# Weighing two key tiles in one block of TensorE, with a fourth buffer of probabilities

## Chip, cores and metric

One core of one Trainium2 chip. The metric is the device time of one execution of the whole program in microseconds (us). Engines: PE is TensorE's matmuls, PEld its weight loads, DVE is VectorE, ACT ScalarE, POOL GpSimd, SP the queue that issues most transfers.

## What is computed

Four transformer layers on x (8 batches x 256 tokens x 128 channels), each an attention and a feed-forward net, with a context of 8 x 1601 tokens x 64 channels. The first and the fourth layer hold a cross attention with 16 heads of 8 channels over all 1601 context tokens:

```python
Q = (x @ Wq.T).reshape(B, 256, 16, 8);  K, V = (z @ Wkv.T) as (B, 1601, 16, 8) each
attn = softmax(einsum('bqhd,bkhd->bhqk', Q, K) * 8 ** -0.5, axis=-1)
O = einsum('bhqk,bkhd->bqhd', attn, V)
```

These two cross attentions are what the change touches; the rest (self attentions, an attention with 16 heads of 32, one with a single head, the feed-forward nets) stays.

## The kernel before

`split_cross` (from line 1772) runs one such attention. It is called twice: for layer 0 with its first queries and keys made ahead, and for layer 3, where it makes its queries itself. The work is cut into 32 **groups** (`NG`): 8 batches of 4 groups with 4 heads each. The 1601 keys of a group are 13 **tiles** (`KT`) of up to 128 keys; a tile of a group is a step u, 416 in all. For every u:

- *fill, scores* (line 1938): four matmuls, one per head, write a tile's scores (128 keys x 256 queries for each head) to one of two score buffers in PSUM. Queries and keys are cut into bf16 pieces, so that the contraction is over 50 rows; two heads lie in the two halves of TensorE's rows.
- *drain, exponential* (line 2018): ScalarE writes exp of the 1024 scores per key to a buffer of probabilities, `probs`; there are three, taken in turn by u. Before it, it waits until the weigh of u-3 is done.
- *weigh* (line 1971): four matmuls in f32, one per head, contract 128 keys: 9 columns of weights (8 value channels and a one, whose sum is the softmax's denominator) against 256 queries. The four heads lie at columns 0, 32, 64 and 96 of the array. The profile shows each as two passes, so a weigh is x8. They add up in one PSUM bank over the 13 tiles of a group.

The softmax's maxima are searched in a pass ahead: *max* (line 1953) multiplies queries by keys the other way round, 32 maxima tiles of 401 keys per group, some 8 steps ahead of the group's own scores; VectorE reduces each (line 2074) from one of two PSUM buffers, the ring: one of two banks, which takes two tiles at once, and one of one bank, used in turn. The maxima are put together (line 2079), cut into bf16 pieces on GpSimd (2115, 2117), transposed on TensorE (*neg*, line 1923), copied by ScalarE (2011) and sent by SP to two further rows of the queries. After a group's last weigh ScalarE copies its output (*take*, 2027), TensorE transposes it (*turn*, 1979), and VectorE divides (2090, 2095). Keys and values of the next batch are projected between (`kproj`, line 1910; `vproj`, line 1916), the keys' pieces cut on GpSimd.

The order is written by a planner, `split_plan` (from line 1687), one list for all engines; each engine runs its own steps of it in that order, with semaphores. A slot is one fill (scores, or a projection, or neg). `LENGTH` gives the planned length of each kind of step; `done` adds these up for two points of each slot, after its fill and after its weigh, and the 32 maxima tiles of a group are put where that sum has reached equal shares. In a slot i the plan runs: fill i, other steps, maxima of the first point, the weigh of the tile that was filled in slot i-2, maxima of the second point, drain of slot i-1.

```python
        if i >= 2 and slots[i - 2][1][0] == "scores":
            u = slots[i - 2][1][1]
            plan.append(("weigh", u))
```

Of the kernel before, what the change touches and what calls it, by code (L numbers as in the profile page):

```python
# [17 lines left out]
ACT = mybir.ActivationFunctionType  # L18
# [4 lines left out]
P = 128  # L23
B = 8
S = 256
# [6 lines left out]
KT = -(-LC // P)  # L32
# [1516 lines left out]
NG = B * GT  # L1549
PER = KT * GT  # L1550
LEAD = 8
LENGTH = dict(scores=0.25, weigh=0.6, qproj=0.9, kproj=0.9, vproj=1.0, neg=0.25)
KT_IN = 16 * 2 * PIECES


# [131 lines left out]
def split_plan(ready):  # L1687

    slots, steps = [], [(-89.0, ("ones",)), (-90.0 if ready else -69.7, ("ctx", 1))]
    if not ready:
        slots += [(-80.0, ("qproj", 0))] + [(-71.0 + c, ("qproj", c)) for c in range(1, 4)]
        steps += [(-69.9, ("qsplit", 0)), (-69.8, ("qsend", 0)), (3, ("qsplit", 1))]
        steps += [(36 + 2.9 * i, ("qsend", 1, i)) for i in range(2 * PIECES)]
    for b in range(B):
        at = PER * (b - 1)  # L1700
        if b >= 2:
            steps.append((at - 34, ("ctx", b)))
        if b >= 1:
            first, apart = (at - 9.5, 1.5) if b == 1 else (at - 22.5, 1)
            slots += [(first + apart * c, ("kproj", b, c)) for c in range(4)]
            steps += [(first + 5.5 + 2.4 * i, ("ksplit", b, i)) for i in range(4)]
            for a in range(GT):
                steps += [(first + 15.5 + 8 * a + 0.65 * i, ("ksend", b, a, i)) for i in range(2 * PIECES)]
        first, apart = (-19.5, 2) if b == 0 else (at + 9.5, 1)
        slots += [(first + apart * s, ("vproj", b, s)) for s in range(5)]  # L1710
    for n in range(NG):
        lo = KT * (n - 1) - LEAD
        hi = lo + KT
        steps += [(hi, ("place", n)), (hi + 0.1, ("cut", n)), (hi + 4.6, ("negsend", n))]
        slots.append((hi + 4.5, ("neg", n)))
    slots = sorted(slots + [(u, ("scores", u)) for u in range(NG * KT)], key=lambda e: e[0])
    steps.sort(key=lambda e: e[0])
    done, work = [], 0.0
    for i, (_, step) in enumerate(slots):
        work += LENGTH[step[0]]  # L1720
        done.append([work])
        if i >= 2 and slots[i - 2][1][0] == "scores":
            work += LENGTH["weigh"]
        done[i].append(work)
    points = [(i, half) for i in range(len(slots)) for half in range(2)]
    items = {point: [] for point in points}
    for n in range(NG):
        lo = KT * (n - 1) - LEAD
        begin, end = [next(i for i in range(len(slots)) if i + 1 == len(slots) or slots[i + 1][0] - 1 > t)
                      for t in (lo, lo + KT)]  # L1730
        mine = [point for point in points if begin <= point[0] < end]
        low, high = done[begin - 1][1] if begin else 0.0, done[end - 1][1]
        for item in range(32):
            at = low + (high - low) * (item + 0.5) / 32
            items[next(point for point in mine if done[point[0]][point[1]] >= at)].append(("max", n, item))
    plan, turns = [], []
    for i, (_, step) in enumerate(slots):
        until = slots[i + 1][0] - 1 if i + 1 < len(slots) else 1e9
        plan.append(("fill",) + step)
        while steps and steps[0][0] < until:  # L1740
            plan.append(steps.pop(0)[1])
        plan += items[i, 0] + turns
        turns = []
        if i >= 2 and slots[i - 2][1][0] == "scores":
            u = slots[i - 2][1][1]
            plan.append(("weigh", u))
            if u % KT == KT - 1:
                turns = [("turn", u // KT)]
        plan += items[i, 1]
        if i:  # L1750
            plan.append(("drain",) + slots[i - 1][1])
        if turns:
            plan.append(("take", turns[0][1]))
    last = NG * KT - 1
    plan += [("weigh", last - 1), ("drain", "scores", last), ("weigh", last), ("take", NG - 1), ("turn", NG - 1)]
    slot = {step: i for i, (_, step) in enumerate(slots)}
    out, ring, skip = [], {}, False
    for step in plan:
        if step[0] == "max":
            if skip:  # L1760
                skip = False
                continue
            wide = len(ring) % 2 == 0 and step[2] < 31
            step = step + (2 if wide else 1,)
            skip = wide
        if step[0] in ("max", "turn"):
            ring[step] = len(ring)
        out.append(step)
    return out, slot, ring


def split_cross(nc, k, scale, tiles, ctx_t, xt, wq, wk, wv, y):

    plan, slot, ring = split_plan(wq is None)
# [4 lines left out]
    with ExitStack() as ctx:  # L1779
        def sb(name, shape, dt=F32):  # L1780
            return k.sb(name, shape, dt, ctx)
# [2 lines left out]
        kt = (tiles.kt0, sb("kt1", [P, GH, LC], BF16))  # L1784
        qf = y.rearrange("p t c -> p (t c)")
        v = sb("v_cur", [P, 2, KT, H * 9])
        pr = sb("probs", [P, 3, 4 * S])
        ot = sb("ot", [P, S])
        rden = sb("rden", [P, QT, 4])
        mx, negm = sb("mx", [P, 2, 32]), sb("negm", [P, 2, 8])  # L1790
# [13 lines left out]
        def wait(eng, sem, count):  # L1804
            if count > 0:
                eng.wait_ge(sem, count)
# [86 lines left out]
        def _(pe):  # L1893
            for step in plan:
                kind = step[0]
                if kind == "fill":
                    kind, of = step[1], step[1:]
                    pair = spair(of)
# [20 lines left out]
                    elif kind == "neg":  # L1919
                        n = of[1]  # L1920
# [21 lines left out]
                elif kind == "max":  # L1942
                    n, i0, count = step[1], step[2], step[3]
                    b, a = n // GT, n % GT
                    if i0 == 0:
                        wait(pe, kt_in[b % 2][a], KT_IN * (b // 2) + KT_IN * (b % 2))
                        if wq is not None:
                            pe.wait_ge(q_in[0 if b < 2 else 1], 16 * 2 * PIECES)
                    wait_ring_reuse(pe, step)
                    for i in range(count):  # L1950
                        j, g, tok, lo = item(n, i0 + i)
                        rows = slice(CC * j, CC * j + PROWS)
                        ins = pe.matmul(bank(step, i)[:, 0:CH], qs[rows, g, tok:tok + P],  # L1953
                                        kt[b % 2][rows, g, lo:lo + CH], start=True, stop=True)
                    ins.then_inc(ring_full, 1)
                elif kind == "weigh":
                    u = step[1]
                    n, t = u // KT, u % KT
                    b, a = n // GT, n % GT
                    m = min(P, LC - P * t)  # L1960
                    if t == 0:
                        if a == 0:
                            wait_drained(pe, ("vproj", b, 4))
                        if n == 0:
                            pe.wait_ge(o_clear, 1)
                        wait(pe, taken, n)
                    wait_drained(pe, ("scores", u))
                    for jj in range(4):
                        j, h = jj % 2, 4 * a + jj
                        at = 2 * S * j + S * (jj // 2)  # L1970
                        ins = pe.matmul(obank[32 * jj:32 * jj + 9, :], v[0:m, b % 2, t, 9 * h:9 * h + 9],  # L1971
                                        pr[0:m, u % 3, at:at + S], start=(t == 0), stop=(t == KT - 1))
                    ins.then_inc(pv_done, 1)
                elif kind == "turn":
                    n = step[1]
                    pe.wait_ge(taken, n + 1)
                    wait_ring_reuse(pe, step)
                    for i in range(QT):
                        ins = pe.transpose(bank(step)[:, P * i:P * i + P], ot[:, P * i:P * i + P], k.ident[:])
                    ins.then_inc(ring_full, 1)  # L1980

        @block.scalar
        def _(act):
            for step in plan:
                kind = step[0]
                if kind == "drain":
# [20 lines left out]
                    elif kind == "neg":  # L2007
                        n = of[1]
                        wait(act, neg_in[n % 2], 32 * (n // 2))
                        wait_filled(act, of)  # L2010
                        act.activation(sg[:, n % 2, :], pair[:, 0, :].bitcast(BF16)[0:8, 0:S],
                                       ACT.Copy).then_inc(s_free, 1)
                    else:
                        u = of[1]
                        m = min(P, LC - P * (u % KT))
                        wait(act, pv_done, u - 2)
                        wait_filled(act, of)
                        act.activation(pr[0:m, u % 3, :], pair[0:m].rearrange("p a n -> p (a n)"), ACT.Exp,  # L2018
                                       scale=scale).then_inc(s_free, 1)
                elif kind == "qsend" and step[1] == 0:  # L2020
                    send_queries(act, 0, (1,))
# [1158 lines left out]
```

## Time and profile before

| | us |
|---|---|
| median of 3 runs | 3841.56 (3839.25 to 3856.53) |
| the profiled execution | 3862.31 |
| its span in the trace | 3860.5 |
| TensorE, VectorE, ScalarE, GpSimd busy in the span | 3281.6, 2320.5, 1797.2, 1139.3 |
| first attention with heads of 8, about | 355 to 974 |
| second, about | 3085 to 3743 |

Busy shares are averages over stages with different limits, so the two attentions are read by themselves. Matmuls are pipelined and their ends are modelled: the start of one against the start of the next tells more than how long one seems to last. An instruction that waits is put down to the semaphore that came last.

### The profile page before, as it was taken

The page shows a single profiled execution, that of the slowest core. Times are in us where ns is not written, and L with a number is a line of the kernel's source. Part 1 is how long each engine was busy: PE and PEld are TensorE (multiplying, and loading weights), DVE is VectorE, ACT ScalarE, POOL GpSimd, SP SyncE. Part 2 cuts the span into 40 slices and gives each one's busy share as a digit, 9 for nine tenths or more (in the row PEclk, how much of TensorE's full clock was granted, in tenths as well). Part 3 has the DMA queues.
Part 4 walks back from the last instruction along what each step waited for, and adds up shares of the span by engine and source line. Part 5 has one row for each costly group of instructions (what it writes and reads, how often), then busy time and mean ns, then how long its engine had stood idle before and what let it go on. Part 6 is the DMA issues. An engine that isn't in the chain of part 4 may idle for free. (4 is left out here: it accounts for less than half of the span.)

```text
span 3860.5 us, 80811 instructions
## 1 busy us (share of the span) xinstructions
PE 3281.6 (85%) x33476; PEld 1659.7 (43%) x33476; DVE 2320.5 (60%) x3829; ACT 1797.2 (47%) x2204; POOL 1139.3 (30%) x797
## 2 busy tenths in 40 slices
PE   6898999999589837999999999978787599999986
PEld 4663333333366523444444444445454233333334
DVE  4455788888466453555555555533334577778876
ACT  2332777778133322444444444443221066777762
POOL 2001111110233252655556655662101121111103
PEclk9996999999599857999999999998887688999987
DMA  4200211110100021000000000000211222121100
GB/s 66 26 2 17 52 32 35 42 42 4 31 9 2 1 60 26 10 2 10 10 10 1 10 10 2 2 1 2 56 47 22 41 49 46 38 46 33 27 2 11
DMA packets 68751, 90.05 MB, mean 23 GB/s; under 512 B 36990, under 2 KB 49322, under 8 KB 68394
## 3 DMA queue, kind: packets, MB, share of 16 engines
q1 hardware_dynamic: 67962, 84.58, 10.8%
q8 instruction: 262, 4.29, 0.5%
q14 instruction: 95, 0.78, 0.1%
q10 hardware_dynamic: 432, 0.39, 0.0%
HBM read 34.31 MB, written 4.33 MB: 10 GB/s over the span
## 5 line engine op out<-in xcount | busy, mean ns | idle before, releaser
L2074 DVE TENSOR_REDUCE mx<-ps 128x2 f32<-128x802 f32 (+1 forms) x1372 | 1020.7, 777 | 251.7 <-PE ps L1953 230.2
L2018 ACT ACTIVATE probs<-ps 128x1024 f32<-128x1024 f32 (+1 forms) x832 | 826.8, 1024 | 210.1 <-PE ps L1938 204.3
L2386 DVE TENSOR_REDUCE mx<-ps 128x3 f32<-128x1203 f32 (+1 forms) x352 | 483.0, 1372 | 478.6 <-PE ps L2282 478.6
L2434 POOL TENSOR_TENSOR sums<-sums,probs 128x2048 f32<-128x2048 f32 x128 | 579.2, 4525 | 143.8 <-ACT probs L2361 129.4
L1971 PE MATMUL ps<-probs,v_cur 128*9 128x256 f32 x6656 | 549.0, 401 | 0.5 <-ACT probs L2018 0.5
L2361 ACT ACTIVATE probs<-ps 128x1024 f32<-128x1024 f32 x384 | 372.2, 1021 | 357.8 <-PE ps L2260 357.7
L1953 PE MATMUL ps<-kt,qs 48*128 48x401 bf16 x2048 | 484.8, 362 | 52.2 <-DVE mx L2074 36.9
L1938 PE MATMUL ps<-qs,kt 50*128 50x256 bf16 (+1 forms) x3328 | 388.1, 288 | 12.4 <-DMA qs<-max_rows 10.1
L2282 PE MATMUL ps<-kt,qt 32*128 32x401 f32 x2048 | 340.2, 556 | 46.7 <-DVE mx L2386 41.1
L1953 PEld LDWEIGHTS ps<-kt,qs 48*128 48x128 bf16 x2048 | 129.3, 95 | 505.2 <-DVE mx L2074 279.6
L2115 POOL CAST max_pieces<-negm 128x8 bf16<-128x8 f32 x64 | 12.2, 191 | 1083.4 <-DVE negm L2079 1083.4
L2260 PE MATMUL ps<-qt,kt 32*128 32x256 f32 (+1 forms) x3328 | 251.7, 375 | 0.0
L2303 PE MATMUL ps<-probs,v_cur 128*32 128x256 f32 (+1 forms) x3328 | 226.9, 386 | 12.9 <-issue 12.7
L1938 PEld LDWEIGHTS ps<-qs,kt 50*128 50x128 bf16 (+1 forms) x3328 | 165.9, 100 | 134.0 <-issue 51.2
L2282 PEld LDWEIGHTS ps<-kt,qt 32*128 32x128 f32 x2048 | 110.9, 186 | 200.9 <-DVE mx L2386 117.4
L2260 PEld LDWEIGHTS ps<-qt,kt 32*128 32x128 f32 (+1 forms) x3328 | 188.5, 181 | 12.1
L844 ACT ACTIVATE probs<-ps 128x768 f32<-128x768 f32 (+1 forms) x128 | 110.4, 914 | 172.1 <-PE ps L777 93.9
L1971 PEld LDWEIGHTS ps<-probs,v_cur 128*9 128x9 f32 x6656 | 103.1, 89 | 184.4 <-issue 130.8
L2303 PEld LDWEIGHTS ps<-probs,v_cur 128*32 128x32 f32 (+1 forms) x3328 | 87.3, 109 | 135.0 <-issue 98.6
L2255 PE MATMUL ps<-max_rows,ones_b 2*128 2x512 bf16 (+1 forms) x896 | 106.2, 371 | 35.7 <-ACT probs L2361 21.7
L878 DVE RECIPROCAL rden<-ps 128x256 f32<-128x256 f32 x64 | 112.3, 1754 | 38.1 <-PE ps L788 38.1
L2431 POOL COPY sums<-probs 128x2048 f32<-128x2048 f32 x32 | 60.5, 1891 | 230.3 <-ACT probs L2361 230.3
(399 smaller groups left out, 4292.0 us busy)
## 6 DMA issues: line engine op xcount, KB each, us to landing
kt<-k SPq DMA_DIRECT2D x680, 50.0 KB
ctx_s<-in_ctx_t SPq DMA_DIRECT2D x16, 400.2 KB, 4.7
ctx_s<-ctx_norm_t SPq DMA_DIRECT2D x16, 400.2 KB, 5.3
kt<-k SPq DMA_DIRECT2D x24, 200.1 KB
ctx_norm_t<-ctx_norm_t SPq DMA_DIRECT2D x8, 400.2 KB, 3.8
ctx_a<-in_ctx_t SPq DMA_DIRECT2D x8, 400.2 KB, 4.2
ctx_b<-in_ctx_t SPq DMA_DIRECT2D x8, 400.2 KB
qs<-q SPq DMA_DIRECT2D x12, 256.0 KB
```

The lines of the kernel that those rows point to most:

```text
L878: dve.reciprocal(rden[:], lbank).then_inc(divided, 1)
L1938: ins = pe.matmul(pair[0:m, j, S * (jj // 2):S * (jj // 2) + S], kt[b % 2][rows, g, P * t:P * t + m], qs[rows, g, S * b:S * b + S], start= ...
L1953: ins = pe.matmul(bank(step, i)[:, 0:CH], qs[rows, g, tok:tok + P], kt[b % 2][rows, g, lo:lo + CH], start=True, stop=True)
L1971: ins = pe.matmul(obank[32 * jj:32 * jj + 9, :], v[0:m, b % 2, t, 9 * h:9 * h + 9], pr[0:m, u % 3, at:at + S], start=(t == 0), stop=(t == ...
L2018: act.activation(pr[0:m, u % 3, :], pair[0:m].rearrange("p a n -> p (a n)"), ACT.Exp, scale=scale).then_inc(s_free, 1)
L2074: dve.tensor_reduce(mx[:, n % 2, i0:i0 + count], src, AX_X, ALU.max).then_inc(freed(step), 1)
L2260: ins = pe.matmul(sbanks[0:m, j, S * i:S * i + S], kt[rows(j), n % 4, P * t:P * t + m], qt[rows(j), b % 2, a, :], start=False, stop=(i == ...
L2282: ins = pe.matmul(rbanks[:, i - 3 * i0, 0:CH], qt[rows(j), b % 2, a, q:q + P], kt[rows(j), n % 4, lo:lo + CH], start=True, stop=True)
L2303: ins = pe.matmul(obank[rows(j), :], v[0:m, n % 2, t, rows(j)], pr[0:m, (NW * n + w) % NPR, j, i, :], start=(t == 0), stop=(t == KT - 1))
L2361: ins = act.activation(pr[:, u % NPR, 2 * f:2 * f + 2, :, :].rearrange("p j i n -> p (j i n)"), sbanks[:, 2 * f:2 * f + 2, :].rearrange("p ...
L2386: dve.tensor_reduce(mx[:, n % 2, 3 * i0:3 * i0 + count], rbanks[:, 0:count, 0:CH], AX_X, ALU.max).then_inc(ring_free, 1)
L2434: pool.tensor_tensor(o, o, p, ALU.add).then_inc(added, 1)
```

## The change

The planner collects tiles that may be weighed in a list and weighs two at once, in one slot, when two are there; when the second belongs to the next group, the first is weighed alone. In slots between, no tile is weighed. A double block is planned at twice 0.45 and 0.15 for a change of the array's shape, where each weigh was planned at 0.6. The probabilities get a fourth buffer (`NPS`), so the exponential of u waits for the weigh of u-4.

```diff
--- before.py
+++ after.py
@@ -1549,7 +1549,8 @@
 NG = B * GT
 PER = KT * GT
 LEAD = 8
-LENGTH = dict(scores=0.25, weigh=0.6, qproj=0.9, kproj=0.9, vproj=1.0, neg=0.25)
+NPS = 4
+LENGTH = dict(scores=0.25, weigh=0.45, turnround=0.15, qproj=0.9, kproj=0.9, vproj=1.0, neg=0.25)
 KT_IN = 16 * 2 * PIECES
 
 
@@ -1715,12 +1716,21 @@
         slots.append((hi + 4.5, ("neg", n)))
     slots = sorted(slots + [(u, ("scores", u)) for u in range(NG * KT)], key=lambda e: e[0])
     steps.sort(key=lambda e: e[0])
+    weighs, ready = [], []
+    for i in range(len(slots)):
+        if i >= 2 and slots[i - 2][1][0] == "scores":
+            ready.append(slots[i - 2][1][1])
+        now = ready[:2] if len(ready) >= 2 else []
+        if now and now[1] % KT == 0:
+            now = now[:1]
+        ready = ready[len(now):]
+        weighs.append(now)
     done, work = [], 0.0
     for i, (_, step) in enumerate(slots):
         work += LENGTH[step[0]]
         done.append([work])
-        if i >= 2 and slots[i - 2][1][0] == "scores":
-            work += LENGTH["weigh"]
+        if weighs[i]:
+            work += LENGTH["weigh"] * len(weighs[i]) + LENGTH["turnround"]
         done[i].append(work)
     points = [(i, half) for i in range(len(slots)) for half in range(2)]
     items = {point: [] for point in points}
@@ -1741,8 +1751,7 @@
             plan.append(steps.pop(0)[1])
         plan += items[i, 0] + turns
         turns = []
-        if i >= 2 and slots[i - 2][1][0] == "scores":
-            u = slots[i - 2][1][1]
+        for u in weighs[i]:
             plan.append(("weigh", u))
             if u % KT == KT - 1:
                 turns = [("turn", u // KT)]
@@ -1752,6 +1761,7 @@
         if turns:
             plan.append(("take", turns[0][1]))
     last = NG * KT - 1
+    plan += [("weigh", u) for u in ready if u < last - 1]
     plan += [("weigh", last - 1), ("drain", "scores", last), ("weigh", last), ("take", NG - 1), ("turn", NG - 1)]
     slot = {step: i for i, (_, step) in enumerate(slots)}
     out, ring, skip = [], {}, False
@@ -1784,7 +1794,7 @@
         kt = (tiles.kt0, sb("kt1", [P, GH, LC], BF16))
         qf = y.rearrange("p t c -> p (t c)")
         v = sb("v_cur", [P, 2, KT, H * 9])
-        pr = sb("probs", [P, 3, 4 * S])
+        pr = sb("probs", [P, NPS, 4 * S])
         ot = sb("ot", [P, S])
         rden = sb("rden", [P, QT, 4])
         mx, negm = sb("mx", [P, 2, 32]), sb("negm", [P, 2, 8])
@@ -1969,7 +1979,7 @@
                         j, h = jj % 2, 4 * a + jj
                         at = 2 * S * j + S * (jj // 2)
                         ins = pe.matmul(obank[32 * jj:32 * jj + 9, :], v[0:m, b % 2, t, 9 * h:9 * h + 9],
-                                        pr[0:m, u % 3, at:at + S], start=(t == 0), stop=(t == KT - 1))
+                                        pr[0:m, u % NPS, at:at + S], start=(t == 0), stop=(t == KT - 1))
                     ins.then_inc(pv_done, 1)
                 elif kind == "turn":
                     n = step[1]
@@ -2013,9 +2023,9 @@
                     else:
                         u = of[1]
                         m = min(P, LC - P * (u % KT))
-                        wait(act, pv_done, u - 2)
+                        wait(act, pv_done, u - NPS + 1)
                         wait_filled(act, of)
-                        act.activation(pr[0:m, u % 3, :], pair[0:m].rearrange("p a n -> p (a n)"), ACT.Exp,
+                        act.activation(pr[0:m, u % NPS, :], pair[0:m].rearrange("p a n -> p (a n)"), ACT.Exp,
                                        scale=scale).then_inc(s_free, 1)
                 elif kind == "qsend" and step[1] == 0:
                     send_queries(act, 0, (1,))
```

## Rows read from the trace of the kernel before

**Rows 1.** Busy time by stretch; columns: stretch, length, each engine (instructions), granted clock, DMA.

```profile
355.00:974.00 619.00, 591.18 (x6316) 207.76 (x6316) 503.61 (x780) 459.42 (x537) 72.96 (x88) 0.96 0.15 33
3085.00:3743.00 658.00, 618.22 (x6335) 213.08 (x6333) 508.39 (x785) 462.89 (x541) 87.63 (x94) 0.91 0.18 35
400.00:950.00 550.00, 525.71 (x5683) 186.77 (x5682) 470.49 (x728) 412.38 (x483) 68.03 (x80) 0.98 0.15 35
3100.00:3340.00 240.00, 222.90 (x2120) 76.43 (x2117) 176.07 (x271) 154.02 (x184) 34.24 (x35) 0.85 0.26 46
```

**Rows 2.** Engines over the whole span: busy us (share), instructions; the profile page.

```profile
PE 3281.6 (85%) x33476; PEld 1659.7 (43%) x33476; DVE 2320.5 (60%) x3829; ACT 1797.2 (47%) x2204; POOL 1139.3 (30%) x797
```

**Rows 3.** Groups by line, 400 to 950 us: count | busy us, mean ns | idle before.

```profile
L2018 ACT ACTIVATE probs<-ps 128x1024 f32<-128x1024 f32 (+1 forms) x372 | 370.6, 1022 | 75.4 <-PE ps L1938 72.4
...
L1971 PEld LDWEIGHTS ps<-probs,v_cur 128*9 128x9 f32 (+1 forms) x2967 | 45.7, 88 | 77.1 <-issue 52.9 <-ACT probs L2018 21.6 <-ACT kf L1998 2.5
...
L2074 DVE TENSOR_REDUCE mx<-ps 128x2 f32<-128x802 f32 x303 | 299.8, 989 | 39.4 <-PE ps L1953 36.0
L2074 DVE TENSOR_REDUCE mx<-ps 128x1 f32<-128x401 f32 x310 | 176.4, 571 | 36.5 <-PE ps L1953 30.8
...
L2090 DVE RECIPROCAL rden<-ps 128x8 f32<-128x8 f32 x29 | 5.9, 202 | 1.0
```

**Rows 4.** Timeline, 603.1 to 607 us: start, us, engine, line, operation, count, [idle before].

```profile
603.25 0.12 PEld L1971 LDWEIGHTS ps<-probs,v_cur 128*9 128x9 f32 x8 [0.21 <-ACT probs L2018]
...
603.80 0.34 PE L1953 MATMUL ps<-kt,qs 48*128 48x401 bf16 x1
...
604.26 0.34 PE L1953 MATMUL ps<-kt,qs 48*128 48x401 bf16 x2
...
604.54 0.62 PE L1971 MATMUL ps<-probs,v_cur 128*9 128x256 f32 x8
...
606.13 0.34 PE L1953 MATMUL ps<-kt,qs 48*128 48x401 bf16 x2
...
606.59 0.99 DVE L2074 TENSOR_REDUCE mx<-ps 128x2 f32<-128x802 f32 x1 [0.38 <-PE ps L1953]
```

**Rows 5.** Timeline of PE, 3718.3 to 3719.3 us, and from 3719.05 us (second pass alone).

```profile
3718.14 0.34 PE L1953 MATMUL ps<-kt,qs 48*128 48x401 bf16 x2
3718.32 0.38 PE L1938 MATMUL ps<-qs,kt 50*128 50x256 bf16 x4
3718.63 0.62 PE L1971 MATMUL ps<-probs,v_cur 128*9 128x256 f32 x8
...
3718.86 0.40 PE L1971 MATMUL ps<-probs,v_cur 128*9 128x256 f32 x4
```

**Rows 6.** Timeline of PE, 477.5 to 479.0 us.

```profile
477.55 0.34 PE L1953 MATMUL ps<-kt,qs 48*128 48x401 bf16 x2
477.83 0.22 PE L1923 MATMUL ps<-identb,max_pieces 128*8 128x128 bf16 x1
...
478.47 0.34 PE L1953 MATMUL ps<-kt,qs 48*128 48x401 bf16 x1
```

**Rows 7.** Timeline of the first attention's tail, 962.1 to 964.5 us.

```profile
961.11 3.77 ACT L2018 ACTIVATE probs<-ps 128x1024 f32<-128x1024 f32 x4
...
963.10 0.39 PE L1938 MATMUL ps<-qs,kt 50*128 50x256 bf16 x4
...
964.02 0.39 PE L1938 MATMUL ps<-qs,kt 50*128 50x256 bf16 x4
```

**Rows 8.** Waits, 400 to 950 us: us in total, times, longest.

```profile
PEld ps L1953 <- DVE mx L2074: 122.8, 292, 0.7
...
PE ps L1953 <- DVE mx L2074: 12.5, 46, 0.6
```

**Rows 9.** Busy time around a fall of the clock, columns as in Rows 1.

```profile
459.50:466.90 7.40, 6.59 (x65) 3.10 (x65) 5.58 (x11) 4.17 (x8) 0.00 (x0) 1.00 0.32 71
466.90:473.70 6.80, 6.80 (x53) 1.99 (x49) 3.33 (x5) 4.39 (x5) 0.00 (x0) 0.50 0.56 128
```

## The prediction

> **What bounds the kernel now.** The table of windows comes first, because the change touches two stretches alone: the two attentions with 16 heads of 8. They take 619 and 658 us of the 3860.5 us span [rows 1], and in them TensorE is busy for 591 and 618 us, against 60% for the whole-span share of VectorE and 47% of ScalarE [rows 2]. In the even part, 400 to 950 us, TensorE is busy for 525.7 of 550 us, VectorE for 470.5 (85.5%), ScalarE for 412.4 (75%), at a granted clock of 0.98 [rows 1]. So TensorE sets the pace there, VectorE follows at 14 points' distance, and no other engine is near. In the second attention the stretch from 3100 to 3340 has less of both clock (0.85) and load [rows 1].
>
> The groups by line, for 400 to 950 us, name VectorE's work: 303 reductions of two tiles at 0.989 us, and 310 of one at 0.571 us; ScalarE has 372 exponentials of 1.02 us [rows 3]. The division of a group's output occurs 29 times [rows 3], so a group (13 key tiles) takes 550/29 = 19.0 us. What VectorE waits for is the maxima's matmuls, 36.0 of 39.4 us idle ahead of the wide reductions and 30.8 of 36.5 ahead of the narrow ones [rows 3].
>
> The timeline then shows how TensorE spends a slot. A weigh starts at 603.25 and the next work of another shape at 603.80: 0.55 us [rows 4]. But its second pass starts 0.23 us after its first (3718.63, 3718.86) [rows 5], so its two passes stream for about 0.44 us, and **0.11 us** goes by before the next maxima matmul. On the way in, a maxima pair at 604.26 is followed by a weigh at 604.54, 0.28 us later [rows 4], where the same pair ahead of a scores block, no change of shape, takes 0.18 us (3718.14 to 3718.32) [rows 5]: **0.10 us** more. So a weigh costs 0.44 us and two pauses, 0.21 us together. That these pauses belong to the change of the array's shape and not to every block is seen where the maxima's transposes (128 rows by 8 columns, shaped like a weigh) stand directly ahead of one: entry at 477.83, 0.28 us after the pair as always, next maxima at 478.47 [rows 6]. The 0.64 us hold both transposes and the weigh, 0.09 more than a weigh alone; a second pair of pauses does not fit into 0.09.
>
> **The change, part by part.** *Fewer blocks.* Two tiles wait until they can be weighed together, but the last tile of a group stands alone (13 is odd): 7 blocks for 13 tiles in place of 13, 6 fewer. Two attentions of 32 groups: 6 x 64 = 384 pairs of pauses. At 0.21 us that is **81 us** of TensorE's time, on the engine that sets the pace.
>
> *The joint inside a double block.* The trace of before has no two weighs back to back without a wait. From below: nothing, as between the passes inside one, where all eight weight loads lie in the first 0.12 us of the block [rows 4]. From above: one weight load in the open, 0.088 us by the mean of its row [rows 3]. I take nothing, since the second four loads are hidden behind the first pass already; the other end goes into the range, and is a rival.
>
> *The later weigh.* The first of two tiles is weighed a slot later. Who waits for it is ScalarE, for a buffer of probabilities: with four, the exponential of tile u needs the weigh of u-4, which stands in the block before. Cost nothing; cover: a whole slot. A copy of a group's output (ScalarE) and its transposes also come a slot later, and move along with the block; the first weigh of the next group waits for that copy as before. Nothing is queued on SP or POOL by the moved step: a weigh issues no transfer.
>
> *Two fills of scores without a weigh between them.* There are two score buffers, so a fill needs the exponential two back. ScalarE alone, in the tail without maxima, does one in 0.92 to 0.94 us (four in 3.77; fills at 963.10 and 964.02) [rows 7]. Two make 1.88 us, while a pair of slots takes 550/186 = 2.96 us all told; with 0.2 us less it is 2.75. So ScalarE stays covered, except in that tail, some 8 slots at each attention's end, where TensorE already goes at ScalarE's pace and gains nothing (4 of 208 pairs, 1.5 us).
>
> *New weights of the planner.* 32 maxima tiles per group are spread by planned work. Per two slots the plan is now 0.25 + 0.25 for fills and 0.9 + 0.15 for the double block, so of some four maxima tiles about 2.7 stand right behind the block, 0.6 behind each fill. The number of matmuls is unchanged; what changes is how even VectorE's supply is. That is the term which gives back.
>
> *What is late next.* VectorE. In 400 to 950 us, 29 x 6 = 174 pairs of pauses, 36.5 us, go away; its idle time falls from 79.5 to 43 us [rows 1]. TensorE now stands idle for 550 - 525.7 = 24.3 us there [rows 1], about half of it shown as waiting for a maxima buffer (12.5 us) [rows 8]. If this wait grows as VectorE's slack shrinks, 79.5/43 = 1.85 times, it becomes 45 us: 20.6 of the 36.5 us saved are given back, 56%. The other end is that none is. I take a third, nearer to none than that estimate, because part of the 24.3 us are waits of fixed length (for ScalarE's copy ahead of the transposes), that do not grow.
>
> *The sum.* 81 x 2/3 = 54 us, from the profiled execution's 3862.3 us (span 3860.5, 1.8 around it): 3808. The median of the runs shown, 3841.56, is 0.9946 of that execution: **3788 us**, 1.4% less. The ends: 81 us (3761) and 81 x 0.44 = 36 us (3806).
>
> **The rivals.** *No give-back:* VectorE's ring stays filled and 81 us arrive, 3761. For it: VectorE would be at 470.5/513.5 = 92%, not full. Against it: it already idles for want of work while TensorE waits for it, so the two are not in step.
>
> *Loads in the open.* Within one weigh the second loads lie under the first pass [rows 4], but all matmuls of a weigh use all 128 rows. If the first load of the second weigh stood open, a joint would cost 0.088 us, and 384 x (0.21 - 0.088) = 47 us would be saved, less a third: 31, so 3811. The Trainium skill, TensorE: Matmul & The Clock Gate, section Part 3 (packing small matmuls), says that a weight load overlaps matmuls in flight only where the row group differs, which speaks for this rival. By that rule the eight loads of one weigh could not lie together under its own first pass either; the trace has them there, so I give it little.
>
> *The ring eats it.* TensorE reaches the maxima after a double block in a bunch, finds both buffers full, and waits as long as it saved: within 0.5% of 3842 (0.5% is about what a measurement of this kernel can tell from no change). For it: there are but two buffers, and already now 292 maxima loads were released last by a reduction [rows 8]. Against: VectorE has 14 points to give before it bounds.
>
> *VectorE runs dry in each double block, slower.* The place is the last maxima step ahead of a block. Reduction starts 0.46 us after its matmul (606.13, 606.59) [rows 4]. The next one comes 0.28 (entry) + 0.88 (two weighs) + 0.11 + 0.46 us after that matmul: 1.27 us from start to start. If only that one step is in the ring, VectorE has 0.99 or 0.57 us of work in it and stands dry for 0.28 or 0.70 us, 0.49 in the mean. A pair of slots holds 470.5/186 = 2.53 us of VectorE's work and 0.43 us of its idle time now. So it decides from 0.43 us of idle time per pair: at 0.49 the pair takes 3.02 against 2.96 us, +0.06 x 384 = 24 us, 3886, by medians 3865. For it: only 0.6 tiles stand ahead of a block. Against: the ring holds two steps, up to 1.56 us of work, and a step that had to wait for its buffer is issued late, with the earlier one still in work.
>
> *Granted clock.* It falls to its lower level, 1.2 GHz, for 6.8 us after the projections of the values (from 466.9; in the 7.4 us before, TensorE was busy for 6.59) [rows 9]. Whether fewer pauses spare some of these I cannot tell; it is in the range, not in the sum.
>
> **How the numbers follow.** The forecast with its give-back 0.50; no give-back 0.12; loads in the open 0.09; ring eats it 0.18; slower 0.11. The first three are faster by over 0.5% (below 3822): 0.71. Within: 0.18. Slower: 0.11. The range takes in the first three and half of the fourth: from somewhat under 3761, for the clock, 3752, to 3838.
>
> **What would show it.** In the changed kernel's timeline 16 weigh matmuls stand together, the second eight 0.44 us after the first (0.53 with a load in the open), the block 1.0 us long to the next shape. The even stretch's group takes 18.1 us in place of 19.0, VectorE's share there is about 90%, the attentions are some 27 us shorter each. Wrong would be: a joint over 0.1 us; VectorE's share at or under 85% with maxima reductions idle for matmuls more than 76 us in 550; TensorE's wait for maxima buffers two times 12.5 us or more; ScalarE idle for a weigh.

## The result: slower, and the profile after

The changed kernel takes 3943.6 us (median of 4) against 3840.4 us: a ratio of **1.0252**, 95% interval 1.0209 to 1.0295, so 103 us (80 to 113) are lost. Its profiled execution has a span of 3928.1 us, the lowest of its runs, where that of before was among the highest of its own; the two traces differ by less than the medians do.

Busy time by stretch in the changed kernel, columns as in [rows 1]: both attentions, from and to the same points of their work as there (6312 and 6335 matmuls, against 6316 and 6335), and 400 to 950 us.

```profile
358.00:1034.00 676.00, 587.03 (x6312) 233.29 (x6310) 501.78 (x780) 451.71 (x537) 72.47 (x88) 0.94 0.14 31
3129.00:3811.00 682.00, 583.04 (x6335) 232.75 (x6333) 505.80 (x784) 456.16 (x541) 87.64 (x94) 0.95 0.17 34
400.00:950.00 550.00, 478.42 (x5085) 191.60 (x5085) 418.79 (x648) 364.10 (x437) 66.81 (x74) 0.94 0.16 34
```

The attentions have grown from 619 and 658 us to about 676 and 682. TensorE is not busier but idler: 478 of 550 us in place of 525.7. VectorE fell from 85.5% to 76%, ScalarE from 75% to 66%. All three engines wait more, and for each other. The mean granted clock of the two attentions, 0.94 and 0.95 against 0.96 and 0.91, moved in both directions, and the groups below that have 1.00 in both kernels lose all the same (5.9 of 6.3 us): it is not the cause.

The same lines by group and the waits, 400 to 950 us of the changed kernel (its line numbers are 10 higher; beside [rows 3] and [rows 8]):

```profile
L2028 ACT ACTIVATE probs<-ps 128x1024 f32<-128x1024 f32 (+1 forms) x332 | 325.0, 1022 | 103.4 <-PE ps L1948 102.4
L2084 DVE TENSOR_REDUCE mx<-ps 128x2 f32<-128x802 f32 x268 | 265.1, 989 | 60.3 <-PE ps L1963 58.5
L2084 DVE TENSOR_REDUCE mx<-ps 128x1 f32<-128x401 f32 x279 | 158.6, 570 | 67.2 <-PE ps L1963 64.2
```

```profile
PE ps L1963 <- DVE mx L2084: 45.8, 102, 1.0
...
PE ps L1948 <- ACT probs L2028: 13.6, 22, 1.0
```

The mean of each instruction is what it was. But TensorE's wait for a maxima buffer rose from 12.5 to 45.8 us while VectorE's wait for maxima rose from 66.8 to 122.7 us; its wait for a score buffer is now 13.6 us, and ScalarE's for scores rose from 72.4 to 102.4 us. Each engine waits for another that waits for it: the buffers between them are handed over at the wrong times.

One cycle of two slots, timeline of the changed kernel, 610 to 613.2 us:

```profile
610.06 0.55 PEld L1981 LDWEIGHTS ps<-probs,v_cur 128*9 128x9 f32 x16 [0.28 <-issue]
610.06 1.05 PE L1981 MATMUL ps<-probs,v_cur 128*9 128x256 f32 x16
...
611.05 0.51 PE L1963 MATMUL ps<-kt,qs 48*128 48x401 bf16 x3
...
611.23 0.55 PE L1948 MATMUL ps<-qs,kt 50*128 50x256 bf16 x4
611.50 1.47 DVE L2084 TENSOR_REDUCE mx<-ps 128x2 f32<-128x802 f32 x2 [0.39 <-PE ps L1963]
...
612.64 0.35 PE L1963 MATMUL ps<-kt,qs 48*128 48x401 bf16 x2 [0.86 <-DVE mx L2084]
...
612.81 0.40 PE L1948 MATMUL ps<-qs,kt 50*128 50x256 bf16 x4
...
613.14 1.05 PE L1981 MATMUL ps<-probs,v_cur 128*9 128x256 f32 x16
```

The double block (x16) takes 0.99 us to the next shape, as forecast, and all its weight loads lie in its first 0.55 us. Behind it TensorE issues three maxima tiles, a pair and a single, which fill both buffers, and a fill. Its third step needs the pair's buffer again. VectorE, which had run dry for 0.39 us, starts on the pair at 611.50, and TensorE stands for 0.86 us until 612.64. The cycle takes 3.08 us.

In other cycles a fill stands. Here two fills follow each other at once (x8), and the next waits 0.97 us for an exponential:

```profile
601.10 0.60 PE L1948 MATMUL ps<-qs,kt 50*128 50x256 bf16 x8
...
602.66 0.39 PE L1948 MATMUL ps<-qs,kt 50*128 50x256 bf16 x4 [0.97 <-ACT probs L2028]
```

What I had averaged over shows in the four groups of one batch, one row each from division to division. First the kernel before, then the changed kernel:

```profile
545.30:562.90 17.60, 17.28 (x197) 5.89 (x199) 13.23 (x21) 14.25 (x16) 0.39 (x2) 0.90 0.29 63
562.90:585.20 22.30, 21.19 (x214) 6.99 (x213) 19.41 (x31) 15.95 (x21) 9.90 (x6) 1.00 0.07 15
585.20:602.60 17.40, 16.42 (x200) 5.46 (x192) 16.28 (x26) 13.68 (x16) 0.40 (x2) 1.00 0.10 22
602.60:623.40 20.80, 19.87 (x213) 8.58 (x207) 17.12 (x28) 14.47 (x19) 0.39 (x2) 1.00 0.26 56
```

```profile
565.50:583.50 18.00, 16.01 (x192) 6.17 (x192) 12.52 (x21) 13.46 (x16) 0.39 (x2) 0.92 0.26 56
583.50:608.50 25.00, 20.93 (x215) 7.64 (x218) 19.90 (x31) 16.01 (x21) 9.90 (x6) 1.00 0.06 14
608.50:627.60 19.10, 15.01 (x194) 6.20 (x190) 15.38 (x26) 13.61 (x16) 0.40 (x2) 1.00 0.09 21
627.60:649.90 22.30, 20.68 (x221) 9.82 (x213) 17.95 (x28) 14.36 (x20) 0.40 (x2) 1.00 0.26 56
```

Before, VectorE is busy for 16.28 of 17.40 us of the third group and for 19.41 of 22.30 us of the second, but for 13.23 of 17.60 us of the first. In the third group VectorE sets the time, though TensorE looks as busy: with short reductions it takes 15.7 us (e2, below). The change lost 0.4, 2.7, 1.7 and 1.5 us: 6.3 us per batch, about the whole loss if all 16 batches (two attentions of 8) lose as much.

Where VectorE's time in the third group goes is seen in its own timeline. Before, it stands idle for maxima three times, 0.78 us in all:

```profile
585.87 3.00 DVE L2074 TENSOR_REDUCE mx<-ps 128x2 f32<-128x802 f32 x4 [0.15 <-PE ps L1953]
589.24 0.99 DVE L2074 TENSOR_REDUCE mx<-ps 128x2 f32<-128x802 f32 x1 [0.38 <-PE ps L1953]
...
595.59 7.10 DVE L2074 TENSOR_REDUCE mx<-ps 128x2 f32<-128x802 f32 x9 [0.25 <-PE ps L1953]
```

In the changed kernel it does so seven times, 3.4 us in all, about once for each of the seven blocks of weighs; three of the seven:

```profile
614.57 1.96 DVE L2084 TENSOR_REDUCE mx<-ps 128x1 f32<-128x401 f32 x3 [0.40 <-PE ps L1963]
617.13 2.50 DVE L2084 TENSOR_REDUCE mx<-ps 128x2 f32<-128x802 f32 x3 [0.60 <-PE ps L1963]
620.42 2.98 DVE L2084 TENSOR_REDUCE mx<-ps 128x1 f32<-128x401 f32 x4 [0.79 <-PE ps L1963]
```

### The profile page after: what moved, and what is told of

Read it like the earlier page. It is cut to its first block and busy times, and to the rows that moved or that the text cites. A ratio compares the mean times of both kernels' runs of the same rounds, so it can differ in the third digit from the quotient of the medians.

```text
span 3928.1 us, 80805 instructions
## 1 busy us (share of the span) xinstructions
PE 3227.9 (82%) x33476; PEld 1698.4 (43%) x33476; DVE 2314.7 (59%) x3827; ACT 1783.4 (45%) x2204; POOL 1139.4 (29%) x797
## 5 line engine op out<-in xcount | busy, mean ns | idle before, releaser
L2028 ACT ACTIVATE probs<-ps 128x1024 f32<-128x1024 f32 (+1 forms) x832 | 815.4, 1023 | 271.1 <-PE ps L1948 267.3
L1963 PE MATMUL ps<-kt,qs 48*128 48x401 bf16 x2048 | 451.2, 359 | 137.2 <-DVE mx L2084 123.7
L1981 PE MATMUL ps<-probs,v_cur 128*9 128x256 f32 x6656 | 475.7, 402 | 0.4 <-ACT probs L2028 0.4
L1948 PE MATMUL ps<-qs,kt 50*128 50x256 bf16 (+1 forms) x3328 | 367.7, 283 | 46.8 <-ACT probs L2028 35.7
L1963 PEld LDWEIGHTS ps<-kt,qs 48*128 48x128 bf16 x2048 | 119.1, 94 | 514.0 <-DVE mx L2084 265.5
L1981 PEld LDWEIGHTS ps<-probs,v_cur 128*9 128x9 f32 x6656 | 144.7, 92 | 190.4 <-issue 90.9
```

The source lines that it names most:

```text
L1948: ins = pe.matmul(pair[0:m, j, S * (jj // 2):S * (jj // 2) + S], kt[b % 2][rows, g, P * t:P * t + m], qs[rows, g, S * b:S * b + S], start= ...
L2028: act.activation(pr[0:m, u % NPS, :], pair[0:m].rearrange("p a n -> p (a n)"), ACT.Exp, scale=scale).then_inc(s_free, 1)
```

## Experiments

Two theories of the loss: **the ring** (the planner bunches the maxima behind the double block, and two buffers can't carry VectorE over it), and **the score buffers** (two fills stand close together, the second waits for the exponential two back). Ratios are to the kernel before on the same chip, with 95% intervals.

**Taking VectorE out of the way** (e1 changed, e2 before): the reductions read 64 columns, about 0.23 us each.

```diff
-                        src = k.ps[:, 4:6, 0:CH]
+                        src = k.ps[:, 4:6, 0:64]
-                        src = bank(step)[:, 0:CH].rearrange(...)
+                        src = bank(step)[:, 0:64].rearrange(...)
-                                       scale=scale).then_inc(s_free, 1)
+                                       scale=scale / 8).then_inc(s_free, 1)
```

> The changed kernel, with VectorE's maxima reductions cut to 64 of their 401 columns (and exponents scaled by 1/8, so that they stay finite): VectorE's ring is out of the way, TensorE and ScalarE have all their work. Ring theory (TensorE waits for VectorE because the maxima stand in a bunch behind the double block): the saved pauses show, 60 to 80 us below the kernel before with the same cut (e2), about 3710 to 3740 us. Score buffer theory (the second of two fills close together waits for the exponential two back): nothing gained against e2, at or above it, about 3790 us or more.

> The kernel before with the same cut of the reductions. Both theories: only its own waits for the ring go, some 24 us of 550 in the even stretch, so 3780 to 3820 us.

Measured: e1 0.9757 (0.9713 to 0.9801), 3754.6 us; e2 **0.9690** (0.9650 to 0.9729), 3729.7 us. The sizes of both expectations missed; e1 above e2 is what the score buffer theory said. The kernel before is 119 us faster with shorter reductions, not the 25 to 65 that were expected. The four groups of the batch in e2, to set beside those of the kernel before above (there the first has a granted clock of 0.90, the others 1.00):

```profile
518.60:534.70 16.10, 15.94 (x197) 5.54 (x201) 4.84 (x22) 14.19 (x18) 0.39 (x2) 1.00 0.37 73
534.70:555.50 20.80, 20.46 (x210) 7.03 (x206) 7.07 (x31) 15.42 (x20) 9.71 (x6) 1.00 0.06 14
555.50:571.20 15.70, 15.62 (x196) 5.55 (x192) 5.97 (x26) 13.61 (x16) 0.60 (x3) 1.00 0.09 21
571.20:590.90 19.70, 19.69 (x211) 8.46 (x203) 6.21 (x26) 14.76 (x20) 0.40 (x2) 1.00 0.28 61
```

They take 72.3 us in place of 78.1, 5.8 less, where TensorE's visible idle time in the batch was 3.35 us (78.1 - 74.75): VectorE held it for more than the profile shows as waiting. That is 93 us for 16 such batches; the rest of the 119 us is not shown to be VectorE's, since the mean granted clock of e2's runs was higher too (0.917 to 0.919, against 0.900 to 0.914). With VectorE out of the way the changed kernel is still 0.7 points (26 us) above. So of 103 us lost, the reductions' length is needed for about 77. The rest fits the score buffers, whose wait is seen in e1 (first row; 400 to 900 us) and not in e2 (second):

```profile
PE ps L1948 <- ACT probs L2028: 24.8, 46, 1.0
```

```profile
PE ps L1938 <- ACT probs L2018: 1.6, 8, 0.3
```

**Taking ScalarE out of the way** (e5 changed, e6 before), and both (e7 changed, e8 before): the exponential covers half its columns.

```diff
-                        act.activation(pr[0:m, u % NPS, :], pair[0:m].rearrange("p a n -> p (a n)"), ACT.Exp,
+                        act.activation(pr[0:m, u % NPS, 0:2 * S], pair[0:m, 0, :], ACT.Exp,
+            dve.memset(pr[:], 1.0).then_inc(o_clear, 1)
...
```

> The changed kernel with each exponential cut to half (512 of 1024 columns, the other half of the probabilities stays 1.0; two heads in four are so left out), VectorE's reductions whole: fills no longer wait for ScalarE, the ring stays as it is. Score buffer theory: most of the loss goes, level with e6 or up to 40 us below it. Ring theory: the loss stays, 50 us or more above e6.

> The kernel before with the same half exponentials (two heads in four left out). Both theories: it hardly waited for ScalarE, 0.5 us in the even stretch, so 3820 to 3845 us.

> The changed kernel with both cuts (64 of 401 columns reduced, half the exponentials; so maxima and two heads in four are not the reference's): TensorE alone is left. Both theories: the 384 pairs of pauses show in full, 65 to 85 us below e8. If a double block does not save its pauses, level with e8.

> The kernel before with both cuts (64 of 401 columns reduced, half the exponentials). Both theories: as e2, 3715 to 3735 us, since nothing there waited for ScalarE.

Measured: e5 1.0126 (1.0085 to 1.0167), e6 0.9951 (0.9921 to 0.9980): 1.75 points apart, so shorter exponentials take a third off the loss, and 67 us stay, as the ring theory said (50 or more). e7 **0.9654** (0.9594 to 0.9715), e8 **0.9632** (0.9585 to 0.9679): level, against both theories' 65 to 85 us. Yet in single cycles the pauses are saved. Two slots with the same work, two maxima steps (three tiles), two fills and two weighs, timeline of e8 and then e7 (e7's rows start two cycles ahead):

```profile
643.72 0.62 PE L1971 MATMUL ps<-probs,v_cur 128*9 128x256 f32 x8
...
645.80 0.40 PE L1971 MATMUL ps<-probs,v_cur 128*9 128x256 f32 x4
```

```profile
645.13 0.51 PE L1963 MATMUL ps<-kt,qs 48*128 48x401 bf16 x3
...
645.58 0.46 DVE L2087 TENSOR_REDUCE mx<-ps 128x1 f32<-128x64 f32 x2 [0.79 <-PE ps L1963]
645.86 0.09 PEld L1963 LDWEIGHTS ps<-kt,qs 48*128 48x128 bf16 x1 [0.28 <-DVE mx L2087]
...
648.80 1.05 PE L1981 MATMUL ps<-probs,v_cur 128*9 128x256 f32 x16
...
650.67 0.62 PE L1981 MATMUL ps<-probs,v_cur 128*9 128x256 f32 x8
```

2.08 us in e8 (643.72 to 645.80), 1.87 us in e7 (648.80 to 650.67): 0.21 less. But two cycles ahead of it, e7's maxima matmul of 645.13 is reduced from 645.58 on, in 0.23 us, and its buffer is refilled at 645.86: a round trip of 0.73 us, 0.5 us of it the matmul itself and the two hand-overs (0.45 us to the reduction's start, 0.05 us from its end). In the bunch behind a double block that is too long even for a tiny reduction. In the planner's list of the kernel before, a weigh (0.55 us) stands between two uses of a buffer of the ring in all but 84 of 716 cases; in that of the changed kernel in all but 289 of 715.

**Hardly any maxima** (e9 changed, e10 before): both cuts, and 4 of 32 maxima tiles.

```diff
-        for item in range(32):
-            at = low + (high - low) * (item + 0.5) / 32
+        for item in range(4):
+            at = low + (high - low) * (item + 0.5) / 4
...
```

> The changed kernel with both cuts and with 4 of the 32 maxima tiles of a group (the other maxima stay 0; 28 of 32 maxima matmuls and reductions and two heads in four are left out): almost no buffer of the ring is needed twice within a block's time. If double blocks save their pauses and the ring's round trip took them back (e7 level with e8): 65 to 90 us below e10. If a double block saves nothing over the whole kernel: level with e10.

> The kernel before with the same omissions (4 of 32 maxima tiles, 64 columns reduced, half the exponentials). Some 18 maxima steps of 0.17 us fewer in each of 64 groups than e8: about 200 us below it, 3490 to 3540 us.

Measured: e9 0.9425 (0.9370 to 0.9479), e10 0.9457 (0.9409 to 0.9506); 13 us apart by medians, the intervals overlap: not the 65 to 90 expected, and both (3608 and 3621 us) far above 3540 us. Another wait had taken the place, of the first scores of a group for the maxima's rows from SP (e9, 400 to 800 us, below; 17.2 us in e10), and the granted clock of 400 to 700 us was 0.87 and 0.89, where e7 and e8 have 1.00. So these two do not tell the theories apart.

```profile
PE ps L1948 <- DMA qs<-max_rows: 24.8, 16, 3.3
```

**Spreading the maxima otherwise** (e3 even; e4 at the points of the kernel before).

```diff
-LENGTH = dict(scores=0.25, weigh=0.45, turnround=0.15, ...
+LENGTH = dict(scores=0.52, weigh=0.2, turnround=0.11, ...            (e3)
+LENGTH = dict(scores=0.25, weigh=0.6, ...                            (e4)
-        if weighs[i]:
-            work += LENGTH["weigh"] * len(weighs[i]) + LENGTH["turnround"]
+        if i >= 2 and slots[i - 2][1][0] == "scores":                (e4)
+            work += LENGTH["weigh"]
```

> The changed kernel with other planned lengths (0.52 a fill, 0.2 a weigh, 0.11 the change of shape), so that of a pair of slots' maxima a third stands behind the first fill, a third behind the double block, a third behind the second fill, in place of 0.6, 2.7 and 0.6 tiles. Ring theory: the waits for VectorE fall to those of the kernel before or less, 3780 to 3810 us. Score buffer theory: the two fills are as close as they were in work, still over 3880 us.

> The changed kernel with the maxima at the points of the kernel before (each weigh counted with 0.6 in its old slot): in a pair of slots 0.6 tiles ahead of the double block, 1.4 behind it, 2.0 behind the second fill. Ring theory: between e3 and the changed kernel, 3800 to 3860 us. Score buffer theory: two more tiles between the close fills, so some 30 us better than the changed kernel, 3900 us or more.

Measured: e3 **1.0092** (1.0061 to 1.0124), 3884 us; e4 1.0252 (1.0211 to 1.0294), 3952.6 us, as slow as the changed kernel. The even spread alone, with the same pairs, wins back 1.6 points, 61 us of 103. But neither run came out as the ring theory had it, and 3884 and 3952.6 us are within the score buffer theory's numbers (over 3880, over 3900), though it also said that e4 would be 30 us better than the changed kernel. TensorE's waits tell more, 400 to 900 us of e3 (two rows), then of e4:

```profile
PE ps L1963 <- DVE mx L2084: 30.4, 67, 0.8
PE ps L1948 <- ACT probs L2028: 7.6, 15, 0.6
```

```profile
PE ps L1963 <- DVE mx L2084: 55.3, 121, 0.8
```

The changed kernel has 42.4 and 12.4 us there, the kernel before 11.1 for the ring. In e4 the wait for a score buffer is gone and the loss is not: it stands at the ring. Why, can be counted in the planner's lists. Of some 710 times that a buffer of the ring is used again in an attention, no weigh and at most one fill stands since its last use 62 times before, 158 times in the changed kernel, 183 in e4 and 80 in e3: e4's spread moved the bunch to another place. What is left in e3 was asked of the next two.

**The even spread with the cuts** (e13 both; e14 exponentials alone): e3's `LENGTH` in e7 and in e5.

> As e7 (both cuts: 64 of 401 columns reduced, half the exponentials), with the even spread of e3. If what keeps e7 level with e8 is the round trip of a maxima buffer, needed again too soon in the bunch behind a double block: 30 to 70 us below e8, about 0.945 to 0.955 of the kernel before, where e8 is 0.963. If double blocks lose in some other way: level with e7, 0.965.

> As e5 (half the exponentials, VectorE's reductions whole), with the even spread of e3. If the bunch alone made TensorE wait for VectorE: level with e6 or below it, 0.985 to 0.997 of the kernel before. If VectorE's share by group is the limit, which no spread within a group mends: between e6 and e5, 1.000 to 1.010.

Measured: e13 **0.9524** (0.9477 to 0.9571), 1.1 points (some 41 us) below e8, as the round trip of a maxima buffer had it (30 to 70), and 1.3 below e7: the spread alone turned level into gain, of half the 81 us. e14 1.0084 (1.0049 to 1.0118), no better than e3, as was expected if VectorE's share by group is the limit: with an even spread ScalarE no longer matters, against the score buffer theory, and pairing still loses while the reductions are whole. The third group of the batch, in e8, e7, e13, and then e14:

```profile
554.80:570.30 15.50, 15.41 (x196) 5.71 (x192) 5.94 (x25) 8.15 (x16) 0.89 (x3) 1.00 0.10 22
```

```profile
556.90:573.00 16.10, 15.23 (x194) 6.03 (x198) 5.49 (x25) 8.19 (x16) 0.40 (x2) 1.00 0.09 21
```

```profile
552.00:567.10 15.10, 14.56 (x196) 6.59 (x192) 5.82 (x25) 8.09 (x16) 0.40 (x2) 1.00 0.11 24
```

```profile
585.00:603.80 18.80, 15.70 (x192) 6.47 (x188) 16.44 (x26) 7.90 (x15) 0.40 (x2) 0.97 0.13 28
```

15.5, 16.1, 15.1 us with short reductions: pairing helps there once it is not bunched. With whole ones the group that had gone at VectorE's pace, 17.4 us, takes 18.8: VectorE has the same 16.4 us of work, and 2.4 us of gaps in place of 1.1.

Where they come from shows in two slots with two weighs, two fills and five maxima tiles. Five tiles are 0.99 + 0.99 + 0.57 = 2.55 us of work for VectorE. The kernel before, then e3:

```profile
588.24 0.62 PE L1971 MATMUL ps<-probs,v_cur 128*9 128x256 f32 x8
...
590.79 0.62 PE L1971 MATMUL ps<-probs,v_cur 128*9 128x256 f32 x8
```

```profile
613.28 1.05 PE L1981 MATMUL ps<-probs,v_cur 128*9 128x256 f32 x16
...
615.77 0.34 PE L1963 MATMUL ps<-kt,qs 48*128 48x401 bf16 x2 [0.55 <-DVE mx L2084]
616.05 0.62 PE L1981 MATMUL ps<-probs,v_cur 128*9 128x256 f32 x8
```

The kernel before does them in 2.55 us, VectorE's pace; e3, with a double block, in 2.77. The median of all such cycles between 400 and 880 us, with no other step of TensorE and at a granted clock of 1.00, is 2.55 and 2.77 us too, and with three tiles 2.09 and 1.87. So, whole reductions given, a pair wins its 0.22 us where VectorE has little work in the cycle and loses as much where VectorE sets its length. With short reductions five tiles take 2.26 us in e8 and 2.06 in e13, by the same medians: there the pair wins in both.

**The fourth buffer alone** (e11), and **pairs in one group of four** (e12), the first of the batch, where VectorE is least busy.

```diff
-        pr = sb("probs", [P, 3, 4 * S])                  (e11, with no pairing)
+        pr = sb("probs", [P, 4, 4 * S])
-        now = ready[:2] if len(ready) >= 2 else []       (e12)
+        now = ready[:1]
+        if now and now[0] // KT % GT == 1 and now[0] % KT < KT - 1:
+            now = ready[:2] if len(ready) >= 2 else []
...
```

> The kernel before with a fourth buffer of probabilities and nothing else. Both theories: level with the kernel before, within 0.3%; the loss is all in the pairing.

> The changed kernel with double blocks in one group of four alone, the one in whose time VectorE is least busy (0.73 to 0.79 in the kernel before), and the maxima there spread evenly over the points as in e3; elsewhere single weighs. If VectorE's share by group decides: that group falls from 17.6 to 19.0 us to about 16.5, the others stay, 3800 to 3830 us. If pairing loses by itself: above the kernel before, 3850 us or more.

Measured: e11 1.0017 (0.9979 to 1.0054), no difference within 0.4%: the loss is all in the pairing and its spread. e12 1.0028 (1.0005 to 1.0051), 3843.4 us: with pairs in a quarter of the groups, next to nothing is lost and nothing is won. It lies between its two forecasts, and the paired group did not fall to 16.5 us. In the batch read above it takes 19.1 us, at a granted clock of 0.82, where the kernel before has 17.6 at 0.90; why, is open.

```profile
544.20:563.30 19.10, 17.62 (x197) 6.67 (x192) 12.09 (x20) 14.07 (x16) 0.39 (x2) 0.82 0.27 58
```

No version here that leaves nothing out beats the kernel before.

## Why the prediction was wrong

*Right:* fewer blocks (382 by the planner's lists, 384 forecast), each worth 0.21 us where nothing else waits (1.87 against 2.08 us in e7 and e8), no weight load in the open (0.99 us for a double block to the next shape, 1.0 was forecast), a fourth buffer that costs nothing by itself (e11), and a later weigh that no exponential is shown waiting for.

*The step that failed* is "What is late next". I read VectorE's slack as 14 points, from one mean of 550 us, and let TensorE's wait for it grow 1.85 times at most, a third of the gain. It grew 3.7 times as far as it shows (12.5 to 45.8 us), and the whole gain and 103 us more were given back; the prediction's own signs of being wrong for this step came (VectorE's share 76%, its reductions idle for 122.7 us). Three errors made that. The mean hid the groups: VectorE had 16.28 of 17.40 us of work in one group of four, 1.1 us of slack where 6 x 0.21 = 1.26 us were to be saved; rows by group, from the same trace, would have shown it. That alone would take the gain and not more; I held VectorE's idle time to shrink by what TensorE saves, where the double blocks made it grow: 3.4 us in that group in place of 0.8. And TensorE's 24.3 us of idle time in 550 understate what it waited: in one batch 3.4 us show, and short reductions took 5.8 off. Presumably a short wait disappears under the modelled ends of matmuls.

*"Nothing" for two fills without a weigh between them* failed as well. I compared ScalarE's 1.88 us of work with 2.75 us of cycle, means again; the second fill can follow the first at once (x8 at 601.10), and a fill waits (13.6 us in the stretch, as far as it shows). 26 us of the loss remain when VectorE is out of the way, none that can be told when both are. It is the smaller part: in e4 and e14 that wait is all but gone (none shown, and 1.1 us, 400 to 900 us) and the loss is not.

*"New weights of the planner"* was named as the term that gives back, with its 2.7 tiles behind the block, and not priced. Where the maxima stand was the largest: 61 of 103 us (e3). The old weights would not have mended it (e4).

*The rivals.* "VectorE runs dry in each double block" had the place and the sign, with a chance of 0.11. Its deciding number, 0.43 us of VectorE's idle time per pair of slots, is now (550 - 418.79)/166 = 0.79. Its price of 24 us was too low: it counted the dry time of one step ahead of the block alone and not TensorE's standing behind it (0.86 us above). That standing is what "the ring eats it" (0.18) described, with a price capped at what a block saves, 0.21 us. "Loads in the open" is out: the second weigh follows the first without a gap. The Trainium skill's rule behind it (TensorE: Matmul & The Clock Gate, Part 3) does not agree with these rows, for weight loads of 9 columns: sixteen of them lie in the first 0.55 us of a block of 0.99.

What stays open: why e13 keeps only half of the 81 us, whether for the ring or for ScalarE's and SP's round trips (e9 and e10 were to tell it and did not), and why e12's paired groups gain nothing.

## What to carry to other kernels

A block on the busiest engine that looks like overhead can be the cover under which buffers come back; before taking it away or doubling it, count how soon each buffer on either side of it is needed again, and compare that with the round trip (its own matmul, the other engine's work, the hand-overs), not with the engines' mean shares. Take the shares by the period of the schedule, here a group and the two slots of a cycle, before calling an engine free. Where steps are bunched, their spread is worth trying first: it moved 61 us here, and the pairing itself won 41 us at best, with both other engines cut short.

## Unexpected in the hardware's behaviour

Going into and out of a block of another array shape takes TensorE about 0.21 us: two slots with three maxima tiles take 2.09 us with two blocks of weighs and 1.87 with one, with five tiles 2.26 and 2.06 (e8, e7 and e13). A PSUM buffer that goes from TensorE to VectorE and back takes some 0.5 us beside VectorE's work on it: 0.73 us from one maxima matmul's start to the refill of its buffer with a reduction of 0.23 us between, the matmul itself included (e7). And an engine's idle time as the profile shows it is no bound on what its partner costs: in one batch TensorE showed 3.4 us of idle time in 78.1, 4%, and shorter reductions took the batch to 72.3, 7% less (e2).
